# The first layer's gates by a comparison and a product in place of one fused operation, in an audio tower of two layers

## Chip, cores and metric

The program runs on one core of a Trainium2 chip. The metric is the device time in microseconds (us) of one execution; lower is better. A change is judged by the median of several executions.

## What is computed

64 sequences of 256 frames with 80 channels go through a tokenizer (five taps, ReLU, batch normalisation) to 252 tokens of width 128, and then through two layers, each with an attention and a mixture of eight experts. The part that the change touches is the choice of experts in the first layer: softmax over eight logits, the two largest kept, all others zero.

```python
logits = xf @ Wr.T + br
probs = jax.nn.softmax(logits, axis=-1)
top2_prob, top2_idx = jax.lax.top_k(probs, 2)
comb = jnp.zeros((n, e), x.dtype).at[jnp.arange(n)[:, None], top2_idx].add(top2_prob)
h = jax.nn.gelu(jnp.einsum('nd,edh->enh', xf, W1) + b1[:, None, :], approximate=False)
o = jnp.einsum('enh,ehd->end', h, W2) + b2[:, None, :]
y = jnp.einsum('ne,end->nd', comb, o)
```

The first layer's attention is softmax attention with a band added to the scores. The second layer has a causal linear attention, then a causal softmax attention with normalised queries and keys, and a dense mixture (all eight experts, softmax gates).

## The kernel before

The sequences are worked in 32 pairs. A pair has 504 tokens: four tiles of 126 tokens, which lie in the partitions of token-major tiles and in the columns of feature-major ones. After a first phase (the tokenizer of all pairs, batch statistics) the pairs go through a software pipeline: while the second layer of one pair runs, the first layer of the next one and the queries and keys of the one after run beside it. The work of a round consists of steps of five kinds: `q` (queries and keys of the first layer), `a` (its attention and the gates), `l` (the linear and causal attention of the second layer), `h` (a chunk of the experts' hidden layer) and `o` (a chunk of their output). In which order the steps stand is written out by hand, one string for each engine (`DVE_ROUND`, `PE_ROUND` and so on). Every engine has a queue of its own, worked strictly in its order; semaphores tie the queues together. A wait therefore holds everything behind it on its engine.

Matrix products in half precision are made of three matmuls (L1282 to L1284), on a high and a low part. For each hidden chunk ScalarE applies the activation (L859), VectorE casts it to the high part (L1247), GpSimd subtracts for the low part (L652), TensorE multiplies, and VectorE adds the expert's output times its gate into the tokens (L1266).

The gates of the first layer are made on VectorE for a pair at once, on tiles of 126 partitions x 4 tiles x 8 experts = 32 numbers in a row. `gate_softmax` (its last line is L981) gives the probabilities `lg[0]`. `gate_top2` compares all pairs of experts (L989 greater, L990 equal), drops ties that stand later (L995), adds (L997) and sums (L999): `lge[0]` then holds how many experts are ahead of each one. L1001 makes the gates, in one scalar-tensor-tensor: (rank < 2) times probability.

```python
dve.wait_ge(S0["ranks5"], n(p + 1))
nc.vector.scalar_tensor_tensor(gates[0:TILE, 0], lge[0][0:TILE], 2.0, lg[0][0:TILE], ALU.is_lt,
                               ALU.mult).then_inc(S0["gate_ready"], 1)
```

TensorE waits for `gate_ready`, turns the gates (L1342), ScalarE copies them out (L715), TensorE multiplies them with the experts' second bias (L1348), and VectorE adds that to the tokens (L1006).

Other steps that stand near L1001 in the rounds belong to the second layer of the pair before. ScalarE copies queries, keys and values out (L811), GpSimd squares queries and keys (L638), VectorE sums the squares (L1186) and adds a small number (L1190), GpSimd takes the power (L642), VectorE scales (L1196). The transfer `qk_spread<-terms` puts the first layer's queries and keys into their place for the next pair; it is issued by SyncE behind VectorE's `qk_lo` (L1026, L1029). In the set-up, ahead of the first phase, GpSimd fills the constant tiles, and later waits for the batch variance (L579).

Of the kernel before, what the change touches and what calls it, by code (L numbers as in the profile page):

```python
# [8 lines left out]
ALU = mybir.AluOpType  # L9
# [10 lines left out]
TILE = SEQ // 2  # L20
TILES = 4
# [7 lines left out]
EXPERTS = 8  # L29
# [209 lines left out]
def program(nc, x_dram, w_dram, vec_dram, row_dram, b2_dram, out_dram):  # L239
    y_dram = nc.dram_tensor("y_scratch", (PAIRS, 128, TOK), F32, kind="Internal").ap()  # L240
    term_dram = [nc.dram_tensor(f"terms{i}", (4, 128, TOK), F16, kind="Internal").ap() for i in range(2)]
    with ExitStack() as ctx:
        def sb(name, shape, dt=F32):
            return ctx.enter_context(nc.sbuf_tensor(name, shape, dt))

        def sem(name):
            return ctx.enter_context(nc.semaphore(name))
# [6 lines left out]
        b2 = sb("b2", [128, 2, TILES, D])  # L254
# [23 lines left out]
        xf_hi = sb("xf_hi", [128, 2, 512], F16)  # L278
        xf_lo = sb("xf_lo", [128, 2, 512], F16)
        gates_all = sb("gates", [128, 2, 128])  # L280
        hid = sb("hid", [128, HIDS, TOK])
        hid_hi = sb("hid_hi", [128, 8, TOK], F16)
        hid_lo = sb("hid_lo", [128, 8, TOK], F16)
# [15 lines left out]
        lg = [sb(f"lg{i}", [128, TILES, EXPERTS]) for i in range(2)]  # L299
        lge = [sb(f"lge{i}", [128, TILES, EXPERTS]) for i in range(2)]  # L300
# [6 lines left out]
        minus_max = sb("minus_max", [128, TILES, GROUPS, 128], F16)  # L307
# [19 lines left out]
        gates = gates_all[:, :, 0:TILES * EXPERTS].rearrange("p a (t e) -> p a t e", t=TILES)  # L327
# [50 lines left out]
        S0 = {name: sem(name + "_0") for name in both.split()}  # L378
        S1 = {name: sem(name + "_1") for name in both.split()}
        SS = (S0, S1)  # L380
        for name in ("z_ready z_turned h_ready v_proj qk_hi_ready qk_lo_ready v_ready s_raw s_max max_turned "
                     "q_shifted st_ready p_exp p_band pv_done o_out o_turned o_rec o_ready wo_ready h_bo h_attn probs "
                     "ranks2 ranks3 ranks4 ranks5").split():
            S0[name] = sem(name)
        for name in ("carried el_exp el_min el_map el_hi el_lo v1_ones v1_proj v1_ready at_raw at_ready off_ready av_done "
                     "den_done den_rec o1_norm wo1_ready h_lin aff_ready qkv_proj qkv_ready sq_ready ss_sum "
# [147 lines left out]
        def _(pool):  # L534
            n = Counter(pool, "wait_pool")
# [5 lines left out]
            def const(instruction):  # L541

                instruction.then_inc(const_done, 1)
                steps[0] += 1
                pool.wait_ge(const_done, steps[0])
# [13 lines left out]
            for view, value in ((ident16[:], 0.0), (qk16[0][:], 0.0), (qk16[1][:], 0.0),  # L559
                                (band[:], float(np.exp(np.float32(0.1)))), (causal[:], 1.0), (causal_add[:], 0.0),  # L560
                                (earlier[:], 1.0), (minus_half[:], -0.5), (v0[:], 1.0),
                                (minus_max[:], 0.0), (gates_all[:], 0.0), (b2[:], 0.0)):
                const(nc.gpsimd.memset(view, value))
            keep(ident16[:], 0, [[-1, 128]], 1, 1.0, ALU.not_equal)

# [97 lines left out]
        def _(act):  # L663
# [187 lines left out]
            def hidden(kind, p, c):  # L851
                _, before = chunks_before(kind, p)
                half = halves_before(kind, p)
                bias = (V_B0, V_B1)[kind] + c
                func = (ACT.Gelu, ACT.Gelu_apprx_tanh)[kind]
                act.wait_ge(F["pre_ready"], n(before + c + 1))

                act.wait_ge(hid_lo_done[c % 2], n(half + (c - HIDS) // 2 + 1))
                nc.scalar.activation(hid[:, c % HIDS], pf[:, c % 2, 0:TOK], func,  # L859
                                     bias=vec[:, bias:bias + 1]).then_inc(F["hid_ready"], 1)  # L860
# [9 lines left out]
        def _(dve):  # L870
            n = Counter(dve, "wait_dve")
# [112 lines left out]
            def gate_top2(p):  # L984
                dve.wait_ge(S0["probs"], n(p + 1))

                mine = lg[0][0:TILE].unsqueeze(3).to_broadcast([TILE, TILES, EXPERTS, EXPERTS])
                other = lg[0][0:TILE].unsqueeze(2).to_broadcast([TILE, TILES, EXPERTS, EXPERTS])
                nc.vector.tensor_tensor(over[0:TILE], other, mine, ALU.is_gt)  # L989
                nc.vector.tensor_tensor(same[0:TILE], other, mine, ALU.is_equal).then_inc(S0["ranks2"], 1)  # L990
                dve.wait_ge(S0["ranks2"], n(p + 1))
                flat = earlier[0:TILE].rearrange("p a b -> p (a b)").unsqueeze(1).to_broadcast(
                    [TILE, TILES, EXPERTS * EXPERTS])
                same_flat = same[0:TILE].rearrange("p t a b -> p t (a b)")
                nc.vector.tensor_tensor(same_flat, same_flat, flat, ALU.mult).then_inc(S0["ranks3"], 1)  # L995
                dve.wait_ge(S0["ranks3"], n(p + 1))
                nc.vector.tensor_tensor(over[0:TILE], over[0:TILE], same[0:TILE], ALU.add).then_inc(S0["ranks4"], 1)  # L997
                dve.wait_ge(S0["ranks4"], n(p + 1))
                nc.vector.tensor_reduce(lge[0][0:TILE], over[0:TILE], AX.X, ALU.add).then_inc(S0["ranks5"], 1)  # L999
                dve.wait_ge(S0["ranks5"], n(p + 1))  # L1000
                nc.vector.scalar_tensor_tensor(gates[0:TILE, 0], lge[0][0:TILE], 2.0, lg[0][0:TILE], ALU.is_lt,  # L1001
                                               ALU.mult).then_inc(S0["gate_ready"], 1)

            def add_bias2(a, p, h_in, h_out):
                dve.wait_ge(SS[a]["bias2_ready"], n(p + 1))
# [34 lines left out]
            def softmax_attention(p):  # L1040
# [51 lines left out]
                gate_softmax(0, p)  # L1092
                yield
                gate_top2(p)
                yield
                yield
# [146 lines left out]
            def hidden(kind, p, c):  # L1243

                _, before = chunks_before(kind, p)
                dve.wait_ge(F["hid_ready"], n(before + c + 1))
                nc.vector.tensor_copy(hid_hi[:, c % 8], hid[:, c % HIDS]).then_inc(F["hid_hi_done"], 1)  # L1247
                if c % 2 == 0 and not POOL_EVEN:
                    dve.wait_ge(F["hid_hi_done"], n(before + c + 1))
                    nc.vector.tensor_tensor(hid_lo[:, c % 8], hid[:, c % HIDS], hid_hi[:, c % 8],  # L1250
                                            ALU.subtract).then_inc(hid_lo_done[0], 1)
# [24 lines left out]
        def _(pe):  # L1276
# [367 lines left out]
            def hidden(kind, p, c):  # L1644

                _, before = chunks_before(kind, p)
                pe.wait_ge(F["hid_ready"], n(before + c - 1))
                if c == 0 and kind == 0:
                    halves_ready(0, p * 3 + 2)
                elif c == 0:  # L1650
                    pe.wait_ge(S1["y_lo"], n(p + 1))
                mm3(pf[:, c % 2, 0:TOK], W(("up0", "up1")[kind], c * 128, 128),
                    (xf_hi[:, kind, 0:TOK], xf_lo[:, kind, 0:TOK])).then_inc(F["pre_ready"], 1)
# [72 lines left out]
```

## Time and profile before

| | |
|---|---|
| median of 3 runs | 4362.26 us (4356.4 to 4363.68) |
| the profiled execution's own time | 4363.7 us |
| its span, first to last instruction | 4362.0 us |
| mean granted TensorE clock | 0.982 of full speed |
| TensorE matmul busy | 4059.1 us, 93% |
| VectorE busy | 3341.9 us, 77% |
| ScalarE busy | 2669.0 us, 61% |
| GpSimd busy | 2539.1 us, 58% |
| chain that ended last, by engine | TensorE 53%, VectorE 25%, ScalarE 6%, GpSimd 5%, issue 4%, DMA 4% |

In the profile DVE is VectorE, ACT is ScalarE, POOL is GpSimd, PE is TensorE and PEld its weight load, SP is SyncE. Times are in us unless marked ns. L12 is line 12 of the kernel. Matmuls overlap, so a busy TensorE need not be at its peak. "Idle before" is the time in which the engine had nothing to run ahead of an instruction, and the name behind it is what ended that time. The chain that ended last is followed backwards from the last instruction, at each step to what released it or to the instruction before it on its engine; "issue" is time for which the profile shows no cause. Releasers come from semaphore events.

### The profile page before, as it was taken

The page shows a single profiled execution, that of the slowest core. Times are in us where ns is not written, and L with a number is a line of the kernel's source. Part 1 is how long each engine was busy: PE and PEld are TensorE (multiplying, and loading weights), DVE is VectorE, ACT ScalarE, POOL GpSimd, SP SyncE. Part 2 cuts the span into 40 slices and gives each one's busy share as a digit, 9 for nine tenths or more (in the row PEclk, how much of TensorE's full clock was granted, in tenths as well). Part 3 has the DMA queues.
Part 4 walks back from the last instruction along what each step waited for, and adds up shares of the span by engine and source line. Part 5 has one row for each costly group of instructions (what it writes and reads, how often), then busy time and mean ns, then how long its engine had stood idle before and what let it go on. Part 6 is the DMA issues. An engine that isn't in the chain of part 4 may idle for free.

```text
span 4362.0 us, 104576 instructions
## 1 busy us (share of the span) xinstructions
PE 4059.1 (93%) x41344; PEld 2996.2 (69%) x41344; DVE 3341.9 (77%) x9262; ACT 2669.0 (61%) x4345; POOL 2539.1 (58%) x2366
## 2 busy tenths in 40 slices
PE   7678999999999999999999999999999999999998
PEld 3346777776777777677777767777777777777666
DVE  3367777877887777788777778878777887777776
ACT  3235666666666666666666666666666666666654
POOL 2134666666666666666656665665666566666655
PEclk9779999999999999999999999999999999999999
DMA  4200000101100010110001011000101100010000
GB/s 143 72 27 27 20 18 26 30 28 30 30 23 18 23 30 28 30 30 25 20 19 30 28 30 30 28 20 16 30 28 30 30 27 19 18 30 28 28 16 6
DMA packets 136937, 127.60 MB, mean 29 GB/s; under 512 B 28928, under 2 KB 135360, under 8 KB 136448
## 3 DMA queue, kind: packets, MB, share of 16 engines
q1 hardware_dynamic: 136448, 120.91, 9.5%
q8 instruction: 328, 5.37, 0.5%
q14 instruction: 161, 1.32, 0.1%
HBM read 71.05 MB, written 49.55 MB: 28 GB/s over the span
## 4 chain that ended last, share of the span: by engine, by line
PE 53%; DVE 25%; ACT 6%; POOL 5%; issue 4%; DMA 4%; SPq 3%; ACTq 0%; DVEq 0%
PE pf L1282 8%; PE pa L1542 8%; PE pf L1284 7%; PE pf L1283 7%; DVE hid_hi L1247 5%; DVE h L1266 5%; PE pa L1428 3%; PE pa L1524 3%; DMA qk_spread<-terms 3%; PE pa L1414 2%; PE pa L1390 2%; PE pa L1282 2%; PE pa L1622 2%; POOL inv_norm L642 2%; SPq L462 2%
## 5 line engine op out<-in xcount | busy, mean ns | idle before, releaser
L652 POOL TENSOR_TENSOR hid_lo<-hid,hid_hi 128x504 f16<-128x504 f32 x1536 | 1836.6, 1210 | 1363.0 <-DVE hid_hi L1247 1363.0
L859 ACT ACTIVATE hid<-pf,vec 128x504 f32<-128x504 f32 x1536 | 1030.6, 681 | 704.1 <-PE pf L1284 547.1
L1282 PE MATMUL pf<-w_hi,hid_hi 128*126 128x128 f16 x6144 | 1133.4, 224 | 46.0 <-DVE h L1266 45.2
L1284 PE MATMUL pf<-w_hi,hid_lo 128*126 128x128 f16 x6144 | 1119.3, 222 | 0.0
L1283 PE MATMUL pf<-w_lo,hid_hi 128*126 128x128 f16 x6144 | 1119.2, 222 | 0.0
L1282 PEld LDWEIGHTS pf<-w_hi,hid_hi 128*126 128x126 f16 x6144 | 846.6, 138 | 187.0 <-DVE h L1266 88.3
L1283 PEld LDWEIGHTS pf<-w_lo,hid_hi 128*126 128x126 f16 x6144 | 847.5, 138 | 40.3 <-issue 1.4
L1284 PEld LDWEIGHTS pf<-w_hi,hid_lo 128*126 128x126 f16 x6144 | 849.1, 138 | 0.0
L1247 DVE CAST hid_hi<-hid 128x504 f16<-128x504 f32 x1536 | 708.3, 486 | 24.1 <-ACT hid L859 23.9
L1266 DVE SCALAR_TENSOR_TENSOR h<-pf,gates,h 126x128 f32<-126x128 f32 x2048 | 572.8, 341 | 78.0 <-PE pf L1284 77.7
L1282 PE MATMUL pf<-xf_hi,w_hi 128*128 128x504 f16 x1536 | 582.3, 379 | 3.7 <-DVE xf_lo L1229 1.5
L1284 PE MATMUL pf<-xf_hi,w_lo 128*128 128x504 f16 x1536 | 580.8, 378 | 0.0
L1283 PE MATMUL pf<-xf_lo,w_hi 128*128 128x504 f16 x1536 | 580.3, 378 | 0.0
L608 POOL TENSOR_TENSOR pt<-pt,band 126x262 f32<-126x262 f32 x512 | 345.0, 698 | 135.8 <-ACT pt L751 133.8
L1542 PE MATMUL pa<-v,pt 126*126 126x65 f32 x3072 | 382.5, 274 | 1.6 <-DVE o L1147 1.2
L751 ACT ACTIVATE pt<-pa 126x504 f32<-126x504 f32 x512 | 274.5, 588 | 157.6 <-PE pa L1414 156.6
L1542 PEld LDWEIGHTS pa<-v,pt 126*126 126x126 f32 x3072 | 360.9, 191 | 2.1 <-issue 2.1
L1047 DVE TENSOR_REDUCE minus_max<-pa 126x2 f16<-126x504 f32 x512 | 325.9, 682 | 45.8 <-PE pa L1390 44.8
L859 ACT ACT_TABLE_LOAD x248 | 318.2, 1283 | 4.4
L1157 DVE TENSOR_TENSOR pt<-pa,causal 126x504 f32<-126x504 f32 x256 | 173.2, 676 | 151.8 <-PE pa L1524 151.8
L1284 PEld LDWEIGHTS pf<-xf_hi,w_lo 128*128 128x128 f16 x1536 | 150.4, 98 | 179.4 <-issue 4.2
L706 ACT ACTIVATE ot_hi<-pa 128x504 f16<-128x504 f32 x192 | 113.3, 590 | 253.1 <-PE pa L1327 253.0
(206 smaller groups left out, 7390.0 us busy)
## 6 DMA issues: line engine op xcount, KB each, us to landing
qk_spread<-terms SPq DMA_DIRECT2D x224, 126.0 KB, 2.5
qk_spread<-terms SPq DMA_DIRECT2D x192, 63.0 KB, 2.3
y_scratch<-hid SPq DMA_DIRECT2D x32, 252.0 KB, 2.1
y_in<-y_scratch SPq DMA_DIRECT2D x32, 252.0 KB, 3.4
terms<-qk_hi SPq DMA_DIRECT2D x32, 252.0 KB, 2.5
terms<-qk_lo SPq DMA_DIRECT2D x32, 252.0 KB, 2.5
qk_spread<-terms SPq DMA_DIRECT2D x32, 252.0 KB
terms<-ot_hi SPq DMA_DIRECT2D x32, 252.0 KB, 2.4
```

The costliest lines, as they stand in the source:

```text
L608: nc.gpsimd.tensor_tensor(strip, strip, band[0:TILE], ALU.mult).then_inc(S0["p_band"], 1)
L652: nc.gpsimd.tensor_tensor(hid_lo[:, c % 8], hid[:, c % HIDS], hid_hi[:, c % 8], ALU.subtract).then_inc(hid_lo_done[c % 2], 1)
L751: nc.scalar.activation(pt[0][0:TILE, i % 8], pa0[0:TILE, i % 2, 0:TOK], ACT.Exp, scale=HEAD ** -0.5).then_inc(S0["p_exp"], 1)
L859: nc.scalar.activation(hid[:, c % HIDS], pf[:, c % 2, 0:TOK], func, bias=vec[:, bias:bias + 1]).then_inc(F["hid_ready"], 1)
L1047: nc.vector.tensor_reduce(minus_max[0:TILE, 2 * b:2 * b + 2, hd // 2, 64 * (hd % 2) + MAX_ROW], pa0[0:TILE, i % 3, 0:TOK].rearrange("p (t ...
L1157: nc.vector.tensor_tensor(pt[1][0:TILE, i % 4].rearrange("p (t q) -> p t q", t=4), pa1[0:TILE, 0, 0:TOK].rearrange("p (t q) -> p t q", t=4 ...
L1247: nc.vector.tensor_copy(hid_hi[:, c % 8], hid[:, c % HIDS]).then_inc(F["hid_hi_done"], 1)
L1266: last = nc.vector.scalar_tensor_tensor(h[0:TILE, i], pf[0:TILE, 2, i * D:(i + 1) * D], gates[0:TILE, kind, i, e:e + 1], h[0:TILE, i], ALU ...
L1282: nc.tensor.matmul(out, ah, bh, start=start, stop=False, skip_group_check=skip)
L1283: nc.tensor.matmul(out, ah, bl, start=False, stop=False, skip_group_check=skip)
L1284: return nc.tensor.matmul(out, al, bh, start=False, stop=stop, skip_group_check=skip)
L1542: last = nc.tensor.matmul(pa1[0:TILE, 1, first:first + wide], factors[:, cols(blk)], v1[0:TILE, 2 * b + kt, hd], start=(t == 0), stop=(t = ...
```

## The change

L1001 is replaced by two tensor-tensor operations with a wait between them. The first compares the ranks with a constant tile of twos and writes 1 or 0 over the ranks; the second multiplies by the probabilities. The tile `two` has the shape of the ranks, [128, 4, 8], and is filled once by GpSimd in the set-up. A semaphore, `ranks6`, ties the two operations together; like the others it gets its starting count from GpSimd.

```diff
+        two = sb("two", [128, TILES, EXPERTS])
...
-                     "ranks2 ranks3 ranks4 ranks5").split():
+                     "ranks2 ranks3 ranks4 ranks5 ranks6").split():
...
-                                (minus_max[:], 0.0), (gates_all[:], 0.0), (b2[:], 0.0)):
+                                (minus_max[:], 0.0), (gates_all[:], 0.0), (two[:], 2.0), (b2[:], 0.0)):
...
                 dve.wait_ge(S0["ranks5"], n(p + 1))
-                nc.vector.scalar_tensor_tensor(gates[0:TILE, 0], lge[0][0:TILE], 2.0, lg[0][0:TILE], ALU.is_lt,
-                                               ALU.mult).then_inc(S0["gate_ready"], 1)
+                nc.vector.tensor_tensor(lge[0][0:TILE], lge[0][0:TILE], two[0:TILE], ALU.is_lt).then_inc(S0["ranks6"], 1)
+                dve.wait_ge(S0["ranks6"], n(p + 1))
+                nc.vector.tensor_tensor(gates[0:TILE, 0], lge[0][0:TILE], lg[0][0:TILE],
+                                        ALU.mult).then_inc(S0["gate_ready"], 1)
```

VectorE's queue in a middle round, before, around the gates of the first layer:

```order
L997 TENSOR_TENSOR ob<-ob 126x256
L999 TENSOR_REDUCE lge<-ob 126x32
L1001 SCALAR_TENSOR_TENSOR gates<-lge,lg 126x32
L1247 CAST hid_hi<-hid 128x504
L1266 SCALAR_TENSOR_TENSOR h<-pf,gates,h 126x128 x4
L1186 TENSOR_REDUCE ss<-o 126x16
L1190 TENSOR_SCALAR ss_eps<-ss 126x16
```

The same place in the changed kernel, whose lines are up to three further down:

```order
L998 TENSOR_TENSOR ob<-ob 126x256
L1000 TENSOR_REDUCE lge<-ob 126x32
L1002 TENSOR_TENSOR lge<-lge,two 126x32
L1004 TENSOR_TENSOR gates<-lge,lg 126x32
L1250 CAST hid_hi<-hid 128x504
L1269 SCALAR_TENSOR_TENSOR h<-pf,gates,h 126x128 x4
L1189 TENSOR_REDUCE ss<-o 126x16
L1193 TENSOR_SCALAR ss_eps<-ss 126x16
```

Nothing changed its place; one instruction stands where one stood, and one follows it. The queues of the other engines hold the same instructions in the same order, but for GpSimd's one fill in the set-up.

## Rows read from the trace of the kernel before

**Rows 1.** The page: busy time of each engine and its share of the span, with instructions.
```profile
PE 4059.1 (93%) x41344; PEld 2996.2 (69%) x41344; DVE 3341.9 (77%) x9262; ACT 2669.0 (61%) x4345; POOL 2539.1 (58%) x2366
```

**Rows 2.** The chain that ended last, 1882 to 1892 us: start, us, what.
```profile
1883.19 0.04 DVE gates L1001
1883.23 1.68 issue
1884.91 0.41 DVE hid_hi L1247
...
1886.35 1.14 DVE ss L1186
...
1887.77 2.91 POOL inv_norm L642
```

**Rows 3.** Instructions of L1001, L970, L981: durations ns min/median/max; who waited.
```profile
L1001 DVE SCALAR_TENSOR_TENSOR gates<-lge,lg x32: 192/1795/1799, 243.9 to 4170.4; 126x32 f32<-126x32 f32 x32
...
  PE pa L1342: 36.6, 31
...
L970 DVE TENSOR_TENSOR lg<-lg,lmax x64: 191/194/911, 240.6 to 4308.2; 126x32 f32<-126x32 f32 x64
...
L981 DVE TENSOR_TENSOR lg<-lge,lmax x32: 192/704/707, 241.6 to 4167.5; 126x32 f32<-126x32 f32 x32
```

**Rows 4.** Timeline of VectorE, 1880 to 1888 us: start, us, line, operation.
```profile
1880.28 0.71 DVE L981 TENSOR_TENSOR lg<-lge,lmax 126x32 f32<-126x32 f32 x1
1881.02 0.43 DVE L989 TENSOR_TENSOR ob<-lg 126x256 f32<-126x256 f32 x1
1881.37 0.42 DVE L990 TENSOR_TENSOR ob<-lg 126x256 f32<-126x256 f32 x1
...
1882.28 0.42 DVE L997 TENSOR_TENSOR ob<-ob 126x256 f32<-126x256 f32 x1
1882.74 0.42 DVE L999 TENSOR_REDUCE lge<-ob 126x32 f32<-126x256 f32 x1
1883.19 1.79 DVE L1001 SCALAR_TENSOR_TENSOR gates<-lge,lg 126x32 f32<-126x32 f32 x1
1884.91 0.41 DVE L1247 CAST hid_hi<-hid 128x504 f16<-128x504 f32 x1
...
1886.28 1.20 DVE L1186 TENSOR_REDUCE ss<-o 126x16 f32<-126x1024 f32 x1
```

**Rows 5.** Timeline of GpSimd, the same stretch; in brackets its idle time before.
```profile
1878.15 2.79 POOL L652 TENSOR_TENSOR hid_lo<-hid,hid_hi 128x504 f16<-128x504 f32 x2 [0.36 <-DVE hid_hi L1247]
1883.05 1.89 POOL L638 TENSOR_TENSOR o<-v 126x1024 f32<-126x1024 f32 x1 [2.11 <-ACT v L811]
1885.40 1.14 POOL L652 TENSOR_TENSOR hid_lo<-hid,hid_hi 128x504 f16<-128x504 f32 x1 [0.46 <-DVE hid_hi L1247]
```

**Rows 6.** Timelines of GpSimd and VectorE in a late round.
```profile
4170.29 1.89 POOL L638 TENSOR_TENSOR o<-v 126x1024 f32<-126x1024 f32 x1 [2.10 <-ACT v L811]
...
4170.44 1.79 DVE L1001 SCALAR_TENSOR_TENSOR gates<-lge,lg 126x32 f32<-126x32 f32 x1
```

**Rows 7.** Timeline of TensorE, 1884 to 1886 us.
```profile
1885.04 0.33 PE L1342 MATMUL pa<-ident,gates 126*128 126x126 f32 x1 [1.21 <-DVE gates L1001]
```

**Rows 8.** Timeline of ScalarE, 1882 to 1888 us.
```profile
1885.40 0.27 ACT L715 COPY gate_t<-pa 128x126 f32<-128x126 f32 x1 [2.44 <-PE pa L1342]
```

**Rows 9.** Stretch 1884 to 1888: busy time by engine, clock, DMA share, GB/s.
```profile
1884.00:1888.00 4.00, 2.61 (x24) 2.10 (x25) 3.96 (x9) 0.72 (x2) 2.31 (x3) 1.00 0.16 44
```

**Rows 10.** The chain around 1926 us.
```profile
1926.02 2.85 DMA qk_spread<-terms
```

**Rows 11.** The chain at the first call (244 us) and behind the second (327 us).
```profile
243.94 0.19 DVE gates L1001
...
328.41 0.42 PE pf L1282
```

**Rows 12.** Timeline of VectorE behind the second call.
```profile
327.81 0.16 DVE L1138 TENSOR_SCALAR den<-pa 126x4 f32<-126x4 f32 x1 [0.62 <-PE pa L1542]
```

**Rows 13.** Waits over the whole span: who for whom, us in total, times, longest.
```profile
POOL bn_rstd L579 <- DVE bn_var L918: 127.4, 1, 127.4
```

## The prediction

> **What bounds the kernel now.** Four views, in this order. The busy times first: TensorE works 93% of the span and VectorE 77% [rows 1], so a cost on VectorE matters only where TensorE, or what feeds it, waits for VectorE. Whether that is so at the changed line is read from the chain of work that ended last. Around a typical call (the one at 1883 us; there are 32) the chain stays on VectorE: L1001, then 1.68 us under "issue", then the cast L1247, the reduction L1186 a little later, and only then GpSimd [rows 2]. So L1001 is on the path.
>
> The third view is the instruction itself. L1001 handles 32 numbers in each of 126 rows. Its shortest duration is 192 ns, its median 1795 [rows 3]. The two short ones are the first two calls, at 244 and 327 us; the other 30 take 1.79 or 1.80 us. The timelines of VectorE and GpSimd together say why: the squares for the causal layer (GpSimd, L638) start at 1883.05 and take 1.89, to 1884.94; L1001 starts at 1883.19 and ends at 1884.98 [rows 4, 5]. It works 0.19 and is held for 1.60 by an instruction of another engine. In a late round the distances are the same to 0.01 us: L638 at 4170.29, L1001 at 4170.44 for 1.79 [rows 6]. The chain counts the 1.68 as "issue" because no semaphore releases it.
>
> The fourth view is who stands still meanwhile. TensorE waits 1.21 us for L1001 before it turns the gates (L1342); ScalarE waits 2.44 for that turn; GpSimd, done at 1884.94, waits 0.46 for the cast queued behind L1001 [rows 5, 7, 8]. After L1001 every one of the four engines starts again from it. Only L638 runs across, and what reads its result, L1186, starts at 1886.28, 1.34 us after L638 ended [rows 4, 5].
>
> **The change part by part.**
> *Removed:* one scalar-tensor-tensor, 32 times, held in 30 of them.
> *Added (1), the comparison:* a tensor-tensor of the same 126x32 numbers in the same place of VectorE's queue, so it starts at the same 1883.19. Does it cost what L1001 cost? A tensor-tensor of this shape takes 191 ns at its shortest and 194 at the median (L970) [rows 3], like L1001's 192. That the operation is a comparison is nothing: a 256-wide is_gt took 0.43 us and a 256-wide add 0.42 [rows 4]. And the hold: L981 is a tensor-tensor with both inputs in SBUF and 32 numbers; it started at 1880.28 while GpSimd worked until 1880.94 (1878.15 + 2.79), and ended at 1880.99. It was held just as L1001 is, and ended 0.05 behind the other engine, L1001 0.04 behind [rows 4, 5]. So the comparison takes L1001's whole place, 1883.19 to 1884.98, and the exchange of the first instruction costs nothing in any of the 32 calls.
> *Added (2), the product:* another 126x32 tensor-tensor, after a wait on the comparison. Its work is 0.19. The gap that such a wait leaves is read from L997 to L999: the first starts at 1882.28 and lasts 0.42, the second starts at 1882.74, so 0.04 [rows 4]. Together 0.23 us. The product finds GpSimd idle: that engine's next instruction starts only after the cast, and the cast is queued behind the product.
> The bounds of (2): two neighbours without a wait, L989 and L990, start 0.35 apart although the first lasts 0.43 [rows 4], so without the cost of a wait it would be 0.19 - 0.08 = 0.11. At the other end, a 32-wide tensor-tensor that is held took 0.70 (median of L981 in the first layer) [rows 3]; with the gap 0.74. I take 0.23, since the conditions of L970 (both inputs in SBUF, GpSimd idle) are those of the product.
> The Trainium skill (VectorE: DVE Perf Modes, The DRAIN you can't avoid) says that a semaphore after each operation of a chain costs nothing extra. By it the product would cost the 0.11 of the unwaited pair, and the sum below would be 31 x 0.11 = 3.4 us. The rows disagree: a waited successor of a 0.42 us tensor-tensor starts 0.46 behind it, an unwaited one 0.35 behind it.
> *What is queued behind.* On VectorE the cast, L1266 and L1186 start 0.23 later; TensorE's turn of the gates, ScalarE's copy and GpSimd's next subtraction too. Since all four engines hang on this one point, nothing overtakes: the rest of the round runs as before, 0.23 later as a whole. What would take it back is work bound by something that does not move, and only a DMA could be that; and in 1884 to 1888 the DMA engines are busy by 0.16 only [rows 9]. The transfer that the chain waits for comes 40 us later, at 1926 [rows 10], and is issued behind VectorE's work of the same round, so it moves too.
> *Where it is free.* The second call, at 326.99, is not on the chain: there TensorE is, matmul after matmul (L1282, 0.42 us) [rows 11]. VectorE idles 0.62 after it, until TensorE is ready [rows 12], which hides 0.23. The first call is on the chain [rows 11]. So 31 calls count, each with its own place like the one shown.
> *Set-up.* GpSimd fills one more tile, 128x32, and raises one more semaphore before the first phase. It later waits 127.4 us for the statistics of the first phase [rows 13]: hidden. If this cover were gone it would be one short instruction, once. No DMA is added; the queues of TensorE, ScalarE and SyncE are as before.
>
> **The sum.** 31 x 0.23 = +7.1 us. The profiled execution took 4363.7 (span 4362.0 and 1.7 around it), so 4370.8; that execution lies 1.4 above the median of the runs, 4362.26, so the median to expect is **4369.4 us**, +0.16%. A measurement of this kernel tells about 0.2%, 8.7 us, from no change; the forecast lies just inside.
>
> **The rivals.**
> *A, neither instruction is held* (a comparison of two tiles goes beside GpSimd where the scalar form did not). Then 30 calls lose 1.60 us and 31 gain 0.23: -48.0 + 7.1 = -40.9, 4321.4. Against it: L981, a tensor-tensor, is held in the same round. For it: only that no row shows a comparison held. 0.04.
> *B, the comparison slips in ahead and the product is held.* L1001 starts only 0.14 us behind L638. If the comparison ran its 0.19 at once, the product would wait until 1884.98: the end of the pair is that of L1001, and 4362 stays. Against it as in A. 0.05.
> *C, slower: the product is held too.* The place is GpSimd's next read of SBUF behind L638. Were it to begin within the 0.04 us between comparison and product, the product would take 0.70 instead of 0.19: 30 x 0.51 = 15.3 on top of 7.1, 4384.7, +0.5%. It decides from the moment at which GpSimd has a subtraction ready that does not depend on the cast behind the product. In the rows it has none (0.46 us idle until that cast) [rows 5]. What may stand in for C is a hold made elsewhere in the round by the shift. 0.06.
> *D, the shift is absorbed.* VectorE is held by GpSimd at other places, L981 for 0.5 us [rows 4]. Where GpSimd did not move and VectorE came 0.23 later, the hold would shrink by as much and the round give it back: 4362. Against it: GpSimd moves too, since it idles for the cast. 0.05.
>
> **How the numbers follow.** The forecast's case has 0.80. Its 7.1 us lies only 1.6 below the 8.7 that can be told, and the runs shown before spread over 7 us (4356.4 to 4363.7); so I share it 0.48 within, 0.31 slower, 0.01 faster. A adds 0.04 to faster, B 0.05 to within, C 0.06 to slower, D 0.04 to within and 0.01 to faster. Together 0.06 faster, 0.57 within 0.2%, 0.37 slower. Range: the bounds 3.4 and 22.9 (31 x 0.74) of the product lie at 4366 and 4385, B and D at 4362, each widened by the scatter of the runs. I take 4359 to 4381, which leaves out A, C's full price and thin tails.
>
> **What the profile of the changed kernel would show.** Right: the comparison at about 1.79 us in 30 calls, the product at about 0.19 in all, 0.04 behind it; TensorE's wait for the gates up from 36.6 us in total over 31 waits [rows 3] to about 43, 0.23 more each; the distance between calls, on average (4170.44 - 1883.19) / 18 = 127.07 us between the two calls shown, 18 rounds apart [rows 4, 6], longer by 0.23; L638 0.14 before the comparison. Wrong: a comparison of 0.19 in the middle rounds (A or B), a product of over 0.3 (C), or rounds that have not grown though the pair takes 2.02 (D).

## The result, and the profile after

The changed kernel is slower: median 4371.78 us (4365.36 to 4374.94, 11 runs) against 4358.38 (4354.58 to 4363.68, 11 runs), ratio 1.0028 with a 95% interval of 1.0019 to 1.0037. That is +12 us, between 8 and 16. The range held the time; the forecast of +7.1, just within 0.2%, was too low, and slower by more than that had a chance of 0.37. Ratios leave out one slow execution of all that follow (kernel with the set-up alone: 4936.97 us at a granted clock of 0.771, the others at 0.98).

The profiled execution took 4366.45 us (span 4364.7), one of the two fastest of the eleven. The timeline of VectorE in the changed kernel, around the gates of the same round as in [rows 4] (start, us, line, operation):

```profile
1883.94 0.42 DVE L1000 TENSOR_REDUCE lge<-ob 126x32 f32<-126x256 f32 x1
1884.40 1.80 DVE L1002 TENSOR_TENSOR lge<-lge,two 126x32 f32<-126x32 f32 x1
1886.23 0.19 DVE L1004 TENSOR_TENSOR gates<-lge,lg 126x32 f32<-126x32 f32 x1
1886.34 0.41 DVE L1250 CAST hid_hi<-hid 128x504 f16<-128x504 f32 x1
...
1887.70 1.21 DVE L1189 TENSOR_REDUCE ss<-o 126x16 f32<-126x1024 f32 x1
```

The timeline of GpSimd there, and that of TensorE:

```profile
1884.25 1.89 POOL L639 TENSOR_TENSOR o<-v 126x1024 f32<-126x1024 f32 x1 [2.11 <-ACT v L812]
1886.83 1.15 POOL L653 TENSOR_TENSOR hid_lo<-hid,hid_hi 128x504 f16<-128x504 f32 x1 [0.69 <-DVE hid_hi L1250]
```

```profile
1886.47 0.33 PE L1345 MATMUL pa<-ident,gates 126*128 126x126 f32 x1 [1.43 <-DVE gates L1004]
```

The comparison is held as the fused operation was, 1.80 us, by the squares that started 0.15 before it. The product takes 0.19 and starts 0.03 behind it. The cast starts 1.94 us behind the first of the two, where it was 1.72. TensorE stands still for 1.43 us instead of 1.21 [rows 7], GpSimd 0.69 instead of 0.46 [rows 5]. The two instructions over the whole span (durations ns min/median/max), and who waited:

```profile
L1004 DVE TENSOR_TENSOR gates<-lge,lg x32: 191/192/193, 243.9 to 4177.3; 126x32 f32<-126x32 f32 x32
...
  PE pa L1345: 43.7, 31
```

```profile
L1002 DVE TENSOR_TENSOR lge<-lge,two x32: 191/1797/1799, 243.7 to 4175.5; 126x32 f32<-126x32 f32 x32
```

TensorE's wait went from 36.6 [rows 3] to 43.7 us, +7.1. So far all is as forecast. What was not forecast stands in the stretches from 4.4 to 6.4 us behind the start of the rank sum (L1000), of four rounds of the changed kernel (busy time by engine, granted clock, DMA share, GB/s):

```profile
740.40:742.40 2.00, 2.00 (x12) 1.21 (x10) 1.37 (x3) 0.44 (x1) 1.15 (x1) 0.50 0.28 71
1888.34:1890.34 2.00, 2.00 (x20) 1.34 (x19) 1.37 (x3) 0.72 (x2) 1.14 (x1) 1.00 0.47 129
2269.37:2271.37 2.00, 2.00 (x13) 1.27 (x12) 1.36 (x3) 0.64 (x1) 1.15 (x1) 0.50 0.48 129
3797.70:3799.70 2.00, 2.00 (x20) 1.34 (x19) 1.37 (x3) 0.72 (x2) 1.14 (x1) 1.00 0.48 129
```

The granted clock is 1.00 in the second and the fourth, and 0.50 in the first and third: TensorE works at 1.2 instead of 2.4 GHz and gets through 12 or 13 matmuls where the others have 20. Read in this way, the 30 rounds from the third call on have this stretch at half clock 9 times in the profiled execution of the changed kernel and 3 times in that of the kernel before, whose third call and the one at 1883 us show the two levels too:

```profile
489.57:491.57 2.00, 2.00 (x11) 1.21 (x10) 1.20 (x3) 0.21 (x1) 1.37 (x1) 0.50 0.48 129
1887.14:1889.14 2.00, 2.00 (x20) 1.35 (x19) 1.14 (x3) 0.96 (x2) 1.37 (x1) 1.00 0.47 129
```

TensorE in one such round of the changed kernel and, below the dots, in one without:

```profile
738.53 0.33 PE L1345 MATMUL pa<-ident,gates 126*128 126x126 f32 x1 [1.44 <-DVE gates L1004]
739.21 1.46 PE L1351 MATMUL pa<-b,gate_t 128*126 128x128 f32 x8 [0.35 <-ACT gate_t L716]
740.46 0.63 PE L1285 MATMUL pf<-xf_hi,w_hi 128*128 128x504 f16 x1
...
1886.47 0.33 PE L1345 MATMUL pa<-ident,gates 126*128 126x126 f32 x1 [1.43 <-DVE gates L1004]
1887.16 1.15 PE L1351 MATMUL pa<-b,gate_t 128*126 128x128 f32 x8 [0.35 <-ACT gate_t L716]
1888.14 0.38 PE L1285 MATMUL pf<-xf_hi,w_hi 128*128 128x504 f16 x1
```

The clock falls while TensorE comes back from its wait for the gates: in the twelve rounds of the two kernels, 0.9 to 1.9 us behind the start of the turn. The Trainium skill (TensorE: Matmul & The Clock Gate, Part 1: The HAM clock gate) states that the engine's clock is gated by how busy it has recently been, with half rate as one setting. The rows agree: 0.50 and 1.00 are the two levels, and the low one comes behind the stand. What a fall costs is the distance between two instructions of VectorE, L1199 and L1220, in the same two rounds:

```profile
744.19 1.22 DVE L1199 TENSOR_TENSOR v<-v,inv_norm 126x1024 f32<-126x1024 f32 x1 [2.38 <-POOL inv_norm L643]
762.18 0.20 DVE L1220 RECIPROCAL inv_sum<-row_sum 126x8 f32<-126x8 f32 x1 [1.14 <-PE pa L1625]
...
1892.13 1.22 DVE L1199 TENSOR_TENSOR v<-v,inv_norm 126x1024 f32<-126x1024 f32 x1 [2.38 <-POOL inv_norm L643]
1908.97 0.20 DVE L1220 RECIPROCAL inv_sum<-row_sum 126x8 f32<-126x8 f32 x1 [1.23 <-PE pa L1625]
```

17.99 against 16.84, and 0.09 more up to the next pair's queries: 1.24 us a fall. The distance has one of these two values in every middle round of both kernels, to 0.03, and the long one exactly where the clock fell. So a first account is 7.1 us for the added instruction and 6 x 1.24 = 7.4 for six more falls, 14.5, where 12 (8 to 16) was measured.

To see what else in a round changed, I split the 29 middle rounds into ten pieces at instructions of VectorE. The mean lengths (us) of the pieces that are spoken of below:

| kernel | rank sum (L999) to L1196 | L1196 to L1217 | queries (L1026) to the first row maximum (L1047) | falls of the clock in 30 |
|---|---|---|---|---|
| before | 7.965 | 16.966 | 9.127 | 3 |
| changed | 8.191 | 17.202 | 8.988 | 9 |
| fused, then ones | 8.191 | 17.164 | 8.913 | 8 |
| three operations | 8.421 | 17.283 | 8.890 | 11 |
| before, filled | 7.965 | 16.852 | 9.062 | 0 |
| before, filled, again | 7.967 | 16.848 | 9.122 | 0 |
| changed, filled | 8.193 | 16.856 | 8.980 | 0 |
| changed, filled, again | 8.192 | 16.851 | 8.990 | 0 |
| three, filled | 8.420 | 16.853 | 8.950 | 0 |
| set-up only | 7.968 | 16.892 | 9.081 | 1 |
| squares behind, before | 7.203 | 16.847 | 9.059 | 0 |
| squares behind, changed | 7.432 | 16.853 | 8.874 | 0 |
| ranks in PSUM, before | 7.863 | 16.845 | 9.167 | 0 |
| ranks in PSUM, changed | 7.862 | 16.845 | 9.006 | 0 |

Each line is one profiled execution. The third of these pieces is the one with the transfer; it scatters from 8.3 to 10.4 in single rounds, and the standard error of such a mean is 0.05 to 0.1. The first is steady to 0.01.

The third piece is shorter with the added operation. Its six means without one are 9.06 to 9.17, the six with one 8.87 to 9.01, with no overlap: 0.14 a round, 4.2 us in 29 rounds, with an uncertainty of about 2.7. Two added operations have 8.89 and 8.95, hardly less. TensorE's wait for the transfer shows the same (waits over the whole span, before and, below the dots, changed):

```profile
PE pa L1390 <- DMA qk_spread<-terms: 34.0, 30, 7.9
...
PE pa L1393 <- DMA qk_spread<-terms: 30.0, 30, 7.9
```

It is 31.4 to 35.3 us in the six traces without the added operation and 26.5 to 30.7 in the six with one. The last of the transfers is issued 5.2 to 5.3 us behind the queries in all of them, so what shortens lies between that issue and the row maximum. Why is not shown. It is not the set-up (9.081 with the set-up alone), and it comes as well where the added operation delays nothing (the pair with the ranks in PSUM). With it the account becomes 7.1 + 7.4 - 4.2 = 10.3, nearer to the 12 measured.

The two profiled executions themselves lie closer together than that. Their 29 middle rounds differ by 8.3 us (6.6 in the first piece, 6.8 in the second, -4.0 in the third, -1.1 in the others), 0.29 a round; outside of them the changed kernel's execution was 5.6 us shorter, so the spans differ by 2.7 only. The account is one of single executions; the 12 us are one of medians.

### The profile page after: what moved, and what is told of

It is laid out like the page before. It is cut to its first block, busy times and chain, and to the rows that moved or that the text cites. A ratio compares the mean times of both kernels' runs of the same rounds, so it can differ in the third digit from the quotient of the medians.

```text
span 4364.7 us, 104610 instructions
## 1 busy us (share of the span) xinstructions
PE 4060.3 (93%) x41344; PEld 2996.5 (69%) x41344; DVE 3345.2 (77%) x9294; ACT 2667.4 (61%) x4345; POOL 2537.8 (58%) x2367
## 4 chain that ended last, share of the span: by engine, by line
PE 54%; DVE 26%; ACT 5%; POOL 5%; DMA 4%; issue 3%; SPq 3%; ACTq 0%; DVEq 0%; POOLq 0%
PE pf L1285 9%; PE pa L1545 8%; PE pf L1287 8%; PE pf L1286 8%; DVE hid_hi L1250 5%; DVE h L1269 5%; PE pa L1431 3%; PE pa L1527 3%; DMA qk_spread<-terms 2%; PE pa L1417 2%; PE pa L1393 2%; PE pa L1285 2%; PE pa L1625 2%; SPq L463 2%; PE pa L1287 2%
```

## The experiments

**Does the number of operations count, or their kind?**

```diff
-                nc.vector.tensor_tensor(lge[0][0:TILE], lge[0][0:TILE], two[0:TILE], ALU.is_lt).then_inc(S0["ranks6"], 1)
+                nc.vector.scalar_tensor_tensor(lge[0][0:TILE], lge[0][0:TILE], 2.0, lg[0][0:TILE], ALU.is_lt,
+                                               ALU.mult).then_inc(S0["ranks6"], 1)
                 dve.wait_ge(S0["ranks6"], n(p + 1))
-                nc.vector.tensor_tensor(gates[0:TILE, 0], lge[0][0:TILE], lg[0][0:TILE],
+                nc.vector.tensor_tensor(gates[0:TILE, 0], lge[0][0:TILE], two[0:TILE],
```

The tile holds 1.0 here. Expected:

> The fused operation stays, writes over the ranks, and a waited product with a tile of ones follows. If only the number of dependent operations in front of the gates counts, the fused one is held 1.79 us in 30 calls, the second takes 0.19, and the time is that of the changed kernel: +7 us from 31 x 0.23, plus some 6 more rounds in which TensorE falls to half clock, 1.24 us each, +14 in all over before. Rival (the comparison of two tiles costs something of its own, in time or by how it meets GpSimd): the time stays within 3 us of before.

Measured: 4369.71 us (6 runs) beside 4359.15 of the kernel before, ratio 1.0026 (1.0015 to 1.0038), and 8 falls: +11, where the changed kernel has +12 and 14 was expected. The fused operation in the first place was held 1.796 us (median), the product took 192 ns, and the piece from the rank sum is 8.191, that of the changed kernel. No difference by the kind can be told; the second, dependent operation costs the time.

**Is it the clock?** Five matmuls on constants are put into TensorE's queue ahead of its wait, in the kernel before and in the changed one. Their output is overwritten by the turned gates.

```diff
             def gate_turn(a, p):
+                if a == 0:
+                    c = COL["up0"]
+                    for _ in range(5):
+                        nc.tensor.matmul(pa0[:, GATES_T[0], 0:TOK], w_hi[:, c:c + 128],
+                                         w_hi[:, c + 128:c + 128 + TOK], start=True, stop=True)
                 pe.wait_ge(SS[a]["gate_ready"], n(p + 1))
```

> The kernel before with five 504-column matmuls on constants, into the bank that the turned gates overwrite, put in TensorE's queue ahead of its wait for the first layer's gates. They fill about 1.05 of the 1.21 us in which TensorE stands still. Clock theory: no round falls to half clock (3 of 30 did), 3 x 1.24 = 3.7 us faster than before. Rival (the long rounds have another cause, a transfer for instance): still about 3 long rounds, time as before or up to 2 us over it.

> The changed kernel with the same five matmuls. Clock theory: no round at half clock (9 of 30 had it), so 9 x 1.24 = 11 us faster than the changed kernel, and slower than the filled kernel before by the added instruction alone, 31 x 0.23 = 7.1 us, so about +3.4 over before. Rival: the long rounds stay, and the time with them, +13 over before.

TensorE in the filled changed kernel (timeline):

```profile
1884.83 1.23 PE L1347 MATMUL pa<-w_hi 128*128 128x504 f16 x5
1886.43 0.33 PE L1350 MATMUL pa<-ident,gates 126*128 126x126 f32 x1 [0.37 <-DVE gates L1004]
```

The wait shrinks to 0.37 here, and in the filled kernel before the timeline shows none. The clock never falls in the 30 rounds of either: L1196 to L1217 is 16.85 or 16.86 in every one. Times: 4359.27 (10 runs) and 4360.57 (10 runs) beside 4359.15, ratios 1.0000 (0.9991 to 1.0010) and 1.0008 (0.9998 to 1.0017). The changed kernel, +12 without the matmuls, is at most +7 with them, though VectorE does the same work (8.193). The clock's part is shown. The 3.7 us that the kernel before should have gained were not seen in the times, though they lie within the interval; in the trace the second piece lost them (16.966 to 16.852).

**More of the same.** A third dependent operation, without and with the filling.

```diff
                 dve.wait_ge(S0["ranks6"], n(p + 1))
+                nc.vector.tensor_tensor(lge[0][0:TILE], lge[0][0:TILE], lge[0][0:TILE], ALU.mult).then_inc(S0["ranks7"], 1)
+                dve.wait_ge(S0["ranks7"], n(p + 1))
```

> The changed kernel with a third dependent operation between the two: the 0/1 tile multiplied by itself, in place, with a wait of its own. Each gate is the same. Sum theory of the prediction: another 31 x 0.23 = 7.1 us on top of the changed kernel. Clock theory: TensorE now stands still 1.66 us instead of 1.43, so more rounds fall to half clock than the 9 of 30, I guess 15; +7.1 and 6 x 1.24 = +7.4, together +14 over the changed kernel, +28 over before.

Measured: 4378.59 us (4 runs), ratio 1.0045 (1.0030 to 1.0060), +19 or 20 instead of +28. The waits of the whole span (who for whom, us in total, times, longest) and the three operations:

```profile
PE pa L1347 <- DVE gates L1006: 50.5, 31, 1.7
```

```profile
1886.08 1.80 DVE L1002 TENSOR_TENSOR lge<-lge,two 126x32 f32<-126x32 f32 x1
1887.92 0.19 DVE L1004 TENSOR_TENSOR lge<-lge 126x32 f32<-126x32 f32 x1
1888.14 0.19 DVE L1006 TENSOR_TENSOR gates<-lge,lg 126x32 f32<-126x32 f32 x1
```

The third costs 0.23 like the second (8.421 after 8.191; TensorE's wait 50.5 after 43.7), but the falls went to 11, not to the 15 that I guessed: 6 more came with the first 0.23 and 2 more with the next, in one profiled execution each. With 11 falls the sum is 14.2 + 8 x 1.24 = 24, still 5 over the measured time; the third piece, 9.127 before and 8.890 here, takes 6.9 of it back. A second series, on one chip with more runs, takes the clock out:

> The filled kernel before once more, as the reference of the next two on the same chip: no round at half clock, the time within 4 us of before. The first measurement gave ratio 1.0000, where 0.9991 (3 x 1.24 = 3.7 us less) was expected.

> The filled changed kernel once more. Sum theory: 31 x 0.23 = 7.1 us over the filled kernel before. Rival (part of the shift is given back where TensorE waits for the transfer of queries and keys; the rounds of the profiles hint at 0.1 each): about 4 us over it, as the first measurement had it (1.3 by the medians, 2.7 by the means).

> The kernel with three dependent operations and the five filling matmuls: the clock's part is gone, only the two added operations are left. Sum theory: 62 x 0.23 = 14.3 us over the filled kernel before, 7.1 over the filled changed one. Rival (given back at the transfer): about 8 and 4. If the clock explained nothing of the kernel with three, this one would be as slow, +19 over before.

Measured beside 4358.6 of the kernel before: 4356.26 (12 runs, ratio 0.9998, 0.9988 to 1.0008), 4359.97 (12 runs, 1.0003, 0.9993 to 1.0012) and 4372.12 (9 runs, 1.0033, 1.0021 to 1.0044). By the medians the first added operation costs 3.7 us and the second 12.2, together 15.9, where the sum theory has 7.1, 7.1 and 14.3. The steady piece grows evenly (7.97, 8.19, 8.42). The uneven halves are in part explained by the third piece: the first operation came out low in both series (1.3 and 3.7 by the medians), and 7.1 less the 4.2 given back at the transfer is 2.9. The rival was right there, but not in saying that every shift gives part back: the second operation gives back next to nothing. For the two together this makes about 10, where 15.9 was measured with an uncertainty of 7; the middle rounds of the profiled executions grew by 12 to 14. That is open, to some 6 us. With three operations the filling gained 0.0012 of the time (5 us, with an uncertainty of 8), where 11 falls should give 13.6; with two it gained 0.0020 to 0.0025 (9 to 11 us) and 9 falls should give 11.

**Is it the set-up?** The tile, its fill and the semaphore alone, none of them used:

> The kernel before with only the set-up of the change: the tile of twos, its fill by GpSimd and the sixth semaphore, none of them used. Sum theory: nothing, within 2 us of before. Rival (tiles behind the new one have moved by 128 bytes, one more semaphore at the start): up to the 3 to 5 us that the sum leaves unexplained.

Measured: 4360.8 us (11 runs), ratio 1.0005 (0.9995 to 1.0016). Nothing that can be told from no change. The rounds have the first and third piece of the kernel before. The clock fell in 1 of the 30, where it fell in 3 in the kernel before with the same stand of 1.21 us: so much do two executions differ.

**Taking the hold away, first way:** GpSimd waits for the gates before it squares.

```diff
+                if isinstance(p, Count) or p + 1 < PAIRS:
+                    pool.wait_ge(S0["gate_ready"], n(p + 2))
                 nc.gpsimd.tensor_tensor(squares[0:TILE], qkv[0:TILE, :, 0:2 * D], qkv[0:TILE, :, 0:2 * D],
```

> The kernel before, with GpSimd waiting for the first layer's gates of the next pair before it squares queries and keys. The fused operation then finds GpSimd idle and takes 0.19 instead of 1.79; the cast and the accumulation behind it start 1.60 earlier. The squares start at about 0.2 us behind the start of the fused operation instead of 0.14 ahead of it and end 2.1 to 2.2 behind it; the sum of squares, until now 3.09 behind, can start at 2.2. So the chain gains about 0.9 us in 30 rounds, -27 us, and TensorE's stand of 1.21 goes, and with it the 3 rounds at half clock, -3.7: -31 us, 0.7% faster than before. Rival: the squares or GpSimd's subtractions behind them become the new bound and hold VectorE elsewhere; then under 10 us are gained.

> The same wait of GpSimd in the changed kernel. The comparison and the product both take 0.19. If the sum of squares waits for the squares, the 0.23 of the second operation moves the squares' start and with it the chain: slower than the same step in the kernel before by 31 x 0.23 = 7.1 us, with no round at half clock in either. If VectorE is at the cast or later when the squares end, the difference is less. Rival: the added operation is worth what it was in the pair before and after, 13 us.

Measured: the kernel before with it 4329.52 us (4 runs) beside 4356.66, ratio 0.9938 (0.9923 to 0.9953); the changed kernel with it 4333.0 (5 runs), 0.9951 (0.9935 to 0.9968). VectorE in the first:

```profile
1870.18 0.19 DVE L1003 SCALAR_TENSOR_TENSOR gates<-lge,lg 126x32 f32<-126x32 f32 x1
1870.30 0.41 DVE L1249 CAST hid_hi<-hid 128x504 f16<-128x504 f32 x1
1870.86 1.13 DVE L1268 SCALAR_TENSOR_TENSOR h<-pf,gates,h 126x128 f32<-126x128 f32 x4
1872.49 1.22 DVE L1188 TENSOR_REDUCE ss<-o 126x16 f32<-126x1024 f32 x1 [0.50 <-POOL o L640]
```

and GpSimd:

```profile
1870.52 1.94 POOL L640 TENSOR_TENSOR o<-v 126x1024 f32<-126x1024 f32 x1 [2.59 <-DVE gates L1003]
1872.42 1.14 POOL L654 TENSOR_TENSOR hid_lo<-hid,hid_hi 128x504 f16<-128x504 f32 x1
```

Nothing is held. The squares start 0.34 behind the fused operation, later than the 0.2 that I put, so the sum of squares starts 2.31 behind it where it was 3.09, and the steady piece lost 0.76, not 0.9. 30 x 0.76 = 23 and the three falls, 3.7, make 26.5; 27 were measured, less than the 31 expected. In the changed kernel the piece is 0.229 longer, 7.432: the added operation pushes the squares, and the chain with them. The difference of the two is 3.5 us by the medians, with few runs; that allows the 7.1 expected, and as well the 2 that are left when the third piece (9.059 and 8.874) is counted.

This is the fastest version of the study, 0.6% faster than the kernel before and 0.9% faster than the changed one.

**Second way:** the ranks go to PSUM, so that the fused operation has one input in SBUF.

```diff
+            ranks = pa0[:, LOGITS[0], 256:256 + TILES * EXPERTS].rearrange("p (t e) -> p t e", t=TILES)
...
-                nc.vector.tensor_reduce(lge[0][0:TILE], over[0:TILE], AX.X, ALU.add).then_inc(S0["ranks5"], 1)
+                nc.vector.tensor_reduce(ranks[0:TILE], over[0:TILE], AX.X, ALU.add).then_inc(S0["ranks5"], 1)
...
-                nc.vector.scalar_tensor_tensor(gates[0:TILE, 0], lge[0][0:TILE], 2.0, lg[0][0:TILE], ALU.is_lt,
+                nc.vector.scalar_tensor_tensor(gates[0:TILE, 0], ranks[0:TILE], 2.0, lg[0][0:TILE], ALU.is_lt,
```

In the changed kernel the comparison reads and writes `ranks`, and the product reads it.

> The kernel before, with the ranks written to PSUM (the bank of the logits, read by then) instead of SBUF, so that the fused operation has one SBUF input only. If it is the second SBUF input that is held by GpSimd's read, the fused operation takes 0.19 with the squares running beside it from 0.14 ahead of it. The sum of squares then starts when the squares end, 1.84 behind the fused operation's start, where it was 3.09: 1.25 x 30 = 37 us gained, and 3.7 from the rounds at half clock, -41 us or -0.9%; more than the 27 of the kernel in which GpSimd waits. Rival (any VectorE operation of this place is held): time as before, 1.79 again.

> The changed kernel with the ranks and the 0/1 tile in PSUM: both of its operations have one SBUF input. Neither is held; together 0.42 us. The sum of squares waits for the squares, which start with ScalarE's copy and not with the gates: VectorE arrives there at 1.49 + 0.23 behind the first operation's start, the squares end at 1.84. So the added operation should cost nothing: the same time as the same step in the kernel before, within 3 us. Rival: it costs its 7.1 us here as well.

Measured: 4350.14 us (11 runs) beside 4357.57, ratio 0.9984 (0.9975 to 0.9993), and 4349.43 (11 runs), 0.9982 (0.9973 to 0.9991). VectorE in the first:

```profile
1880.22 0.19 DVE L1003 SCALAR_TENSOR_TENSOR gates<-pa,lg 126x32 f32<-126x32 f32 x1
1880.33 1.91 DVE L1249 CAST hid_hi<-hid 128x504 f16<-128x504 f32 x1
```

and in the second:

```profile
1881.93 0.20 DVE L1004 TENSOR_TENSOR pa<-pa,two 126x32 f32<-126x32 f32 x1
1882.16 0.19 DVE L1006 TENSOR_TENSOR gates<-pa,lg 126x32 f32<-126x32 f32 x1
1882.27 1.67 DVE L1252 CAST hid_hi<-hid 128x504 f16<-128x504 f32 x1
```

with GpSimd's squares in the first and in the second:

```profile
1880.07 1.89 POOL L638 TENSOR_TENSOR o<-v 126x1024 f32<-126x1024 f32 x1 [2.10 <-ACT v L811]
```

```profile
1881.77 1.89 POOL L639 TENSOR_TENSOR o<-v 126x1024 f32<-126x1024 f32 x1 [2.10 <-ACT v L812]
```

The operation with one SBUF input is not held: 0.19 us, 0.15 behind the start of the squares, where the same operation with two took 1.79. The Trainium skill (SBUF — State Buffer, Who interferes with whom) states that of two SBUF inputs the second comes through an interface shared with GpSimd's reads, and that a cast in its fast mode, which reads through both, contends with GpSimd too. The rows agree with both halves, though the trace doesn't name the mode of a cast. The second was my miss: the cast behind took the hold over, 1.91 us instead of 0.41. It ends 2.17 behind the start of the squares, where it ended 2.27 behind it before (1885.32 and 1883.05 [rows 4, 5]), so 0.1 a round is gained and not 1.25. With the falls gone (TensorE gets its gates at once) that makes 30 x 0.10 + 3.7 = 6.7 us; 7 (3 to 11) were measured, not the 41 expected.

And here the change costs nothing, as expected: the comparison and the product end, then the cast is held until the same moment, 2.17 behind the start of the squares. The steady piece is 7.862 beside 7.863, the times are 0.7 us apart. The added 0.23 is hidden where another instruction behind it is held until a fixed moment; it is paid where it comes after the end of the hold, and where the squares themselves wait for it.

## Why the prediction was right and wrong

- *The comparison takes the fused operation's whole place, hold included:* right, 1.80 us in the 30 calls, 0.19 in the first two. Rivals A and B fell with it.
- *The product is 0.23:* right, 0.19 and 0.03 to 0.04; the steady piece grew by 0.226, by 0.229 with GpSimd waiting, and by 0.23 again for a third. The 0.11 without the cost of a wait fell. The Trainium skill (VectorE: DVE Perf Modes, The DRAIN you can't avoid) measured waits that cost nothing on a chain of eight tensor_copy; the prediction had taken that for a rule on every operation. No product was held, so rival C fell.
- *31 calls count, +7.1 us:* TensorE's wait grew by just that. The times don't show it alone: without the clock's part, one added operation cost 1.3 and 3.7 us, two 15.9 where the sum is 14.3.
- *"Since all four engines hang on this one point, nothing overtakes: the rest of the round runs as before, 0.23 later as a whole":* this step failed, twice. The order in the queues did stay, and the last transfer is issued at the same distance; but the time of a round does not depend on order alone. First, TensorE stands still 0.23 longer there, and the clock fell to half in 9 rounds instead of 3, each 1.24 us. The piece in which this shows had two values already in the kernel before, the long one 3 times in 29; the prediction looked at a round that had the short one. Six falls are 7.4 us, a term that the sum put at nothing. Second, TensorE's wait for the transfer, which "moves too", became shorter by 0.14 a round, 4 us, for a reason not shown. The two together lift the forecast of 7.1 to 10.3, over what a measurement tells from no change.
- *Rival D* (the hold elsewhere shrinks) fell as named: L981, L982 in the changed kernel, took 704 ns at the median in both. What was given back came at the transfer.
- *The range and 4369.4:* the range held, with some luck. The absolute forecast lies only 2.4 us under the measured 4371.78 because it started from a median of three runs, 4362.26, where eleven gave 4358.38. The start was 4 us too high and the shift 6 us too small.
- *What the profile would show:* all signs came as named, but for the distance between calls, which grew by 0.29 on average instead of 0.23.
- *The set-up:* nothing, as put.

Open: what decides in a single round whether the clock falls, since 1.43 us of standing went before a round with and one without; why the transfer's piece is shorter by 0.14 with one added operation and hardly more with two; and some 6 us of the filled kernel with three operations.

## What to carry to other kernels

Read what holds a small instruction before swapping it: here 1.6 of 1.8 us belonged to another engine, a second instruction took its full 0.23 a round behind the hold and was free ahead of one. A hold has to be taken off the whole stretch, here by moving GpSimd's read (27 us gained); taking it off one instruction hands it to the next. Where TensorE waits for a small engine, look over all rounds for the granted clock behind the wait: here 0.23 us more of standing, 30 times, cost about as much again through the clock.

## What was not expected of the hardware

TensorE's granted clock fell from 1.00 to 0.50 behind a stand of 1.21 us in 3 and 1 of 30 rounds (two kernels), of 1.43 us in 9 and 8, of 1.66 us in 11, and in none of 30 where five matmuls left 0.60 us of it, 0.37 or none. A fall delayed this kernel by 1.24 us. Stands of equal length (1.43 and 1.44) came with and without it.
